# Three of four batches' experts sorted by token slots inside the MLP groups, instead of dense passes

## The reference

```python
x = x + tanh(g_xattn[0]) * two_way_attention(layernorm(x), ctx)   # with a sigmoid gate
x = x + tanh(g_ffn[0])   * experts(layernorm(x))                  # 8 linear experts, top 2
x = x + tanh(g_xattn[1]) * cross_attention(layernorm(x), ctx)
x = x + tanh(g_ffn[1])   * mlp(layernorm(x))                      # 256 -> 1024 -> 1024 -> 1024 -> 256

# experts: probs = softmax(x @ Wr); the two largest are taken, not renormalised
# out = sum over the two of  p_e * (x @ Wi[e]) @ Wo[e]
# mlp: h = silu(x@w1*s1) * (x@w2*s2); h = gelu(h@h1*s3); h = gelu(h@h2*s4); h @ w3 * s5
```

## Time and profile before

| what | value |
|---|---|
| runs | 1141.81, 1142.21, 1142.49 us (median 1142.21) |
| profiled execution | 1142.89 us, span 1141.0 us |
| PE busy | 1093.0 us (96%), 5194 products |
| DVE, ACT, POOL busy | 534.4, 439.9, 206.3 us |
| granted TensorE clock, mean | 0.983 |
| moved | 121.39 MB, mean 106 GB/s |

### The profile page before, as it was taken

How to read it: one execution, slowest core, us unless ns; L and a number is a source line. 1 busy time by engine, 2 the same in 40 slices (tenths; PEclk the granted TensorE clock), 3 DMA queues, 4 the chain that set the end, 5 groups by cost and what they waited for, 6 DMA issues and landing times.

```text
span 1141.0 us, 14295 instructions
## 1 busy us (share of the span) xinstructions
PE 1093.0 (96%) x5194; PEld 865.1 (76%) x5194; DVE 534.4 (47%) x1420; ACT 439.9 (39%) x820; POOL 206.3 (18%) x336
## 2 busy tenths in 40 slices
PE   7989979899999989999999999999999999999997
PEld 5757768677777767887887788788788788788886
DVE  6567666777777662243334235135135223332411
ACT  1344441112222244445435435535534443543531
POOL 0015552200000111121121122112112112112111
PEclk9989988999999989999999999999999999999999
DMA  9200000112222324443445345345444345443551
GB/s 342 99 1 1 1 1 1 37 56 74 74 74 75 128 61 116 137 148 111 129 120 157 113 127 166 111 136 151 117 131 148 111 129 149 128 115 116 176 146 40
DMA packets 32698, 121.39 MB, mean 106 GB/s; under 512 B 4222, under 2 KB 4478, under 8 KB 31736
## 3 DMA queue, kind: packets, MB, share of 16 engines
q0 software_dynamic: 25344, 92.29, 27.7%
q1 hardware_dynamic: 6456, 25.22, 6.6%
q10 hardware_dynamic: 832, 3.02, 0.7%
HBM read 116.31 MB, written 4.19 MB: 106 GB/s over the span
## 4 chain that ended last, share of the span: by engine, by line
PE 84%; DVE 6%; ACT 4%; issue 3%; POOL 1%; DMA 1%; DVEq 0%; SPq 0%; POOLq 0%; ACTq 0%
PE psum L849 53%; PE psum L728 13%; PE psum L751 2%; PE psum L738 1%; PE psum L463 1%; PE psum L550 1%; PE psum L526 1%; PE psum L777 1%; PE psum L759 1%; PE psum L706 1%; PE psum L564 1%; DVE x_residual L1539 1%; DMA x_residual<-in_x 1%; PE psum L580 1%; ACT L1118 1%
## 5 line engine op out<-in xcount | busy, mean ns | idle before, releaser
L849 PE MATMUL psum<-hidden_a_high,mlp_pieces 128*128 128x512 f32 x512 | 207.4, 405 | 0.0
L849 PE MATMUL psum<-hidden_b_high,mlp_pieces 128*128 128x512 f32 x512 | 200.6, 392 | 0.0
L849 PE MATMUL psum<-hidden_a_low,mlp_pieces 128*128 128x512 f32 x512 | 199.7, 390 | 0.0
L849 PE MATMUL psum<-hidden_b_low,mlp_pieces 128*128 128x512 f32 x512 | 199.2, 389 | 0.0
L1769 POOL DMA_DIRECT2D mlp_pieces<-in_mlp x176 | 94.5, 538 | 534.1 <-PE psum L849 528.3
L1653 DVE TENSOR_TENSOR hidden_a_low<-hidden_a,hidden_a_high 128x512 fp32r<-128x512 f32 x128 | 88.0, 688 | 173.8 <-ACT hidden_a_high L1170 173.0
L1653 DVE TENSOR_TENSOR hidden_b_low<-hidden_b,hidden_b_high 128x512 fp32r<-128x512 f32 x64 | 44.3, 693 | 221.0 <-ACT hidden_b_high L1170 221.0
L1539 DVE SCALAR_TENSOR_TENSOR x_residual<-psum,expert_weight,x_residual 128x256 f32 (+1 forms) x256 | 107.2, 476 | 41.1 <-PE psum L728 40.3
L849 PEld LDWEIGHTS psum<-hidden_a_high,mlp_pieces 128*128 128x128 f32 x512 | 96.2, 188 | 24.1 <-issue 3.6
L849 PEld LDWEIGHTS psum<-hidden_a_low,mlp_pieces 128*128 128x128 f32 x512 | 96.2, 188 | 22.1 <-issue 3.4
L849 PEld LDWEIGHTS psum<-hidden_b_low,mlp_pieces 128*128 128x128 f32 x512 | 96.2, 188 | 19.9
(11 more groups left out here) (211 smaller groups left out, 1624.5 us busy)
## 6 DMA issues: line engine op xcount, KB each, us to landing
mlp_pieces<-in_mlp POOLq DMA_DIRECT2D x176, 512.0 KB, 3.8
mlp_piece_to_examine<-in_mlp SPq DMA_DIRECT2D x22, 512.0 KB, 3.6
x_residual<-in_x SPq DMA_DIRECT2D x4, 1024.0 KB, 22.9
out<-x_residual SPq DMA_DIRECT2D x8, 512.0 KB, 3.4
expert_in<-in_Wi SPq DMA_DIRECT2D x1, 2048.0 KB, 16.7
expert_out<-in_Wo SPq DMA_DIRECT2D x1, 2048.0 KB, 21.3
attention_weights<-in_aw ACTq DMA_DIRECT2D x1, 1280.0 KB, 11.0
attention_weights<-in_aw ACTq DMA_DIRECT2D x2, 256.0 KB, 4.2
```

Source lines behind the costliest of these rows:

```text
L849: last = mm(o, a, b, start=(k == 0 and i == 0), stop=(k == n_k - 1 and i == len(parts) - 1))
```

## The change

Only batch 0 (groups 0 and 1, `ND` = 2) goes through the dense passes; the loop with passes 1 to 6 is gone. Batches 1, 2 and 3 (`NSB` = 3) are done inside MLP groups 0, 2 and 4 (`routed_in(n)`), with the batch that follows the one the MLP is at:

- In w12, DVE normalises the batch's eight tiles (`r_norm`, c = 0 to 3), PE transposes them in pairs (`r_turn`, c = 1 to 4) and makes the router logits in fp32 (`r_logits`, c = 2 to 5, `wrb`); DVE copies them (`r_copy`, c = 6), finds the two largest and marks them (`r_max`, c = 7, `r_mask` after the last low).
- In h1, PE makes the running count of tokens per expert with a triangular matrix (`r_rank`, after chunk 0); DVE makes each token's two weights (`r_coef`) and two slot numbers (`r_rank`, chunk 1, `r_tiles`, chunk 3). Each expert's slots are rounded up to tiles of 128: at most 23 tiles (`EB`) for 2048 slots. POOL writes each tile's normalised rows to the slots in HBM (`scatter`, 16 indirect DMAs of 128 rows of 1 KB, four ahead of each of the piece loads 6 to 9). The slot buffers, 3072 rows of 1 KB for each of three batches, are filled with zeros at the start by SP.
- In h2, SP loads the slots in chunks of four tiles into two buffers (`load_slots`). From chunk 1 on PE transposes pairs of slot tiles (`s_turn`) and, two pairs for each of the chunks 2 to 7, multiplies each tile with its own expert's matrix (`s_experts`), whose column is loaded from SBUF into a register (`s_columns`). ACT and DVE make high and low parts (`s_high`, `s_low`), ACT saves the result and issues its store to HBM (`s_save`).
- At the group's end POOL gathers each token's two rows for group n + 2, and inside group n + 1 for group n + 3 (`gather`, 8 indirect DMAs each); DVE adds them with their weights in group n + 1 (`add_rows`, `measure_rows`). In groups 1, 3 and 5 stage C is four chunks later (`turn_after`).
- The examination takes 16 pieces from three buffers and the last 6 from the ring itself. It lies in pass 0 and the last pass, and its result comes after the last pass.

```diff
-            with pe.Fori(0, NG // 2 - 1) as i:
-                b_pass(2 * i + 1, 1, 2 * i)
-                b_pass(2 * i + 2, 0, 2 * i + 1)
-            b_last_pass(NG - 1, 1)
+            b_last_pass(ND - 1, 1)
...
+                        if s is not None and 1 <= c <= 4:
+                            r_turn(s, c - 1)
+                        if s is not None and 2 <= c <= 5:
+                            r_logits(s, c - 2)
...
+                            if s is not None and layer == 0 and c == 0:
+                                r_rank(s)
+                            if s is not None and layer == 1:
+                                if c == 1:
+                                    columns = s_columns(s, 0)
+                                    s_turn(s * PAIRS)
+                                    s_turn(s * PAIRS + 1)
+                                for i in pairs_at(c):
+                                    if i == PAIRS // 2:
+                                        columns = s_columns(s, 1)
+                                    if i + 2 < PAIRS:
+                                        s_turn(s * PAIRS + i + 2)
+                                    s_experts(s * PAIRS + i, columns)
...
+                def s_experts(q, columns):
+                    pe.wait_ge(xsl_r, q + 1)
...
+                    for i in range(pair_tiles(q)):
+                        v = columns[(q % PAIRS * 2 + i) % 12]
+                        o = ps[:, 2 + q % 2, i * D:(i + 1) * D]
+                        t = slice(i * P, (i + 1) * P)
+                        for k in range(KC):
+                            mm(o, xsh[:, q % 2, k, t], wexp_h[:, k, bass.ds(v, D)], start=(k == 0), stop=False)
+                            mm(o, xsl[:, q % 2, k, t], wexp_h[:, k, bass.ds(v, D)], start=False, stop=False)
+                            last = mm(o, xsh[:, q % 2, k, t], wexp_l[:, k, bass.ds(v, D)], start=False,
+                                      stop=(k == KC - 1))
+                    last.then_inc(ye_ps, 1)
...
 # DVE's group, w12
+                        if s is not None and c < 4:
+                            r_norm(s, c)
+                        if s is not None and c == 6:
+                            r_copy(s)
+                        if s is not None and c == 7:
+                            r_max(s)
                     low(HC - 1, ha_f, ha_h, ha_l, 3 * HC * n + HC)
+                    if s is not None:
+                        r_mask(s)
...
 # POOL
+            def scatter(s, tiles):
+                for j in tiles:
+                    for i in range(2):
+                        pool.indirect_dma_start(
+                            slots[s], bass.IndirectOffsetOnAxis(ap=slot[:, s * JT + j, i:i + 1], axis=0),
+                            xm[:, j, :], None).then_inc(sc_done[s], 16)
...
+                    if s is not None and 6 <= piece < 10:
+                        if piece == 6:
+                            pool.wait_ge(ix_r, s + 1)
+                            pool.wait_ge(fill_done, 16 * NSB)
+                        scatter(s, (2 * piece - 12, 2 * piece - 11))
+                    if a is not None and piece == 8:
+                        pool.wait_ge(cb_r, JT * a + G)
+                        gather(n + 2)
...
+                if s is not None:
+                    for h in range(2):
+                        pool.wait_ge(st_done[h], 16 * NCK // 2 * (s + 1))
+                    gather(n + 2)
...
 # SP
+            def load_slots(s):
+                sp.wait_ge(sc_done[s], 16 * 2 * JT)
+                for c in range(NCK * s, NCK * (s + 1)):
+                    if c % NCK >= 2:
+                        sp.wait_ge(xt_ps, pairs_before(c - 2) + 2)
+                    n = chunk_tiles(c)
+                    sp.dma_start(xs[:, c % 2, 0:n, :], chunk_rows(slots, c, n)).then_inc(xs_in[c % 2], 16)
```

More of the change, by code:

```diff
@@ L52 @@
 RING = 6
+ND = 2
+NSB = B - 1
+EB = 23
+CHUNK = 4
+NCK = -(-EB // CHUNK)
+ROWS_B = NCK * CHUNK * P
+PAIRS = -(-EB // 2)
+XT0 = NT + G * ND
 SLICE = PIECE
@@ L157, in program @@
+        iota = place("weights", "tile_numbers", [1, EB])
+        eid = place("weights", "tile_expert_column", [1, NSB, EB], I32)
+        tri = place("weights", "triangle", [P, P])
+        slot = place("weights", "slots_of_tokens", [P, NSB * JT, 2], I32)
+        cab = place("weights", "weights_of_slots", [P, NSB * JT, 2])
         wk = room["work"][0]
@@ new lines, in r_logits @@
+                def r_logits(s, p):
+                    pe.wait_ge(rx_r, 4 * s + p + 1)
+                    if s == 0 and p == 0:
+                        pe.wait_ge(tri_in, 48)
+                    for i in range(2):
+                        j = 2 * p + i
+                        for k in range(KC):
+                            last = mm(ps[:, 0, j * E:(j + 1) * E], xmT[:, p % 2, k, i * P:(i + 1) * P],
+                                      wrb[:, k, :], start=(k == 0), stop=(k == KC - 1))
+                    last.then_inc(rl_b, 1)
@@ new lines, in s_columns @@
+                def s_columns(s, half):
+                    a, e = (0, 12) if half == 0 else (12, EB)
+                    pe.wait_ge(eid_r, s + 1)
+                    return nc.values_load_multi_w_load_instructions(
+                        eid[0:1, s, a:e], engines=[pe.engine], min_val=0, max_val=(E - 1) * D,
+                        skip_runtime_bounds_check_because="the column is a minimum with that of the last expert")[1]
+                def s_experts(q, columns):
+                    pe.wait_ge(xsl_r, q + 1)
+                    if q % PAIRS >= 2:
+                        pe.wait_ge(ye_r, q - 1)
+                    else:
+                        pe.wait_ge(xupc, 1 + G * (2 * (q // PAIRS) + 2))
+                    for i in range(pair_tiles(q)):
+                        v = columns[(q % PAIRS * 2 + i) % 12]
+                        o = ps[:, 2 + q % 2, i * D:(i + 1) * D]
+                        t = slice(i * P, (i + 1) * P)
+                        for k in range(KC):
+                            mm(o, xsh[:, q % 2, k, t], wexp_h[:, k, bass.ds(v, D)], start=(k == 0), stop=False)
[3 more added lines that the diff above has]
+                    last.then_inc(ye_ps, 1)
@@ new lines, in r_max @@
+            def r_max(s):
+                dve.wait_ge(lc_r, s + 1)
+                for j in range(JT):
+                    st.mark(dve.max(rtop[:, j, :], rlg[:, j, 0:E]))
+                st.wait()
+                dve.tensor_tensor(rlsub[:], rlg[:, :, 0:E], rtop[:, :, 0:1].broadcast_to([P, JT, E]), ALU.subtract
+                                  ).then_inc(le_r, 1)
+                st.link(dve.tensor_copy(rwant[:, :, 0:2], rtop[:, :, 0:2]))
+                for j in range(JT):
+                    st.mark(dve.match_replace(rmarked[:, j, :], rwant[:, j, :], rlg[:, j, :], TAKEN))
@@ L1637, in norm, with measure_rows @@
+            def measure_rows(g):
+                dve.wait_ge(cb_r, G * (g - 1))
+                for j in range(G):
+                    measure(G * g + j, j)
+                aggregate(G * g, G, 0, stats)
             def norm(n):
@@ L1703, in _ @@
             norm(0)
[L1704 removed]
+            b_end(ND - 1)
             steps_before = st.start + st.n
@@ L1866 @@
     d["out"] = nc.dram_tensor("out", (NG, P, G, D), F32, kind="ExternalOutput").ap()
+    for n in ("slots", "yrows"):
+        d[n] = [nc.dram_tensor(f"{n}_{b}", (ROWS_B, D), F32, kind="Internal").ap() for b in range(NSB)]
     program(nc, d)
```

446 lines of the change are left out of this document (377 added, 69 removed).

## The result

The changed kernel takes **1084.99 us** (median of 4 runs, 1082.92 to 1085.43) against 1142.01 (4 runs, 1141.37 to 1142.49). The ratio is 0.9497, 95% interval 0.9481 to 0.9514: 57.0 us gained. The profiled execution took 1084.55 us, its span is 1082.6. Forecast from 1142.89 was -62.1; it came to -58.3.

A forecast was written before the change was run, and what follows sets the result against it. PE (TensorE) was taken to bound the kernel. From 1142.89 us: -158.0 + 81.6 + 8.3 + 2 + 0 + 4.5 + 1 - 1.5 = -62.1, so 1080.8, forecast 1080; 1068 to 1092 at chance 0.50, 1064 to 1115 about 0.8.

The forecast's parts named there:

- The two sides of the sum: PE time removed with six dense passes, -158.0 us, against PE work added in three routed groups, +81.6 us.
- Six passes, -158.0: Six of eight dense passes go at 26.33 us each; pass 0 and the last, with its cross attention, stay.
- the ends, +1: Before the MLP: the weights' check sum now follows the last pass, mostly covered by DVE's norms releasing the turn; +1 us.
- 27.2 us of PE work a group, +81.6: Groups 0, 2 and 4: expert products, slot and x transposes, router logits and rank products on PE, 27.2 us each.
- DVE's r_max, +8.3: First h1 chunk: PE's k = 7 waits about 2.3 us for r_max, then 0.45 for r_mask; 2.75 in three groups.
- Clock, +2: PE, idle in the routed groups' stalls, can lose its clock: 0.7 us each, +2 in all, bounds 0 and 2.
- Slots, 0: Routing, scatter and slot load finish at T + 45, nearly 4 us before h2 wants them; S, POOL's indirect-DMA time, 1.1 us.
- one of the prediction's own signs of being wrong: Signs listed: expert products spaced near 0.2, PE idle before s_turn until slot rows come, or routed-group clock below 1.00.
- The 47 us: Scatters: extra cost if POOL were held 2.3 us for each whole indirect DMA; the prediction set it aside, citing the trace.
- Registers, +4.5: Expert products on PE: loading and addressing by weight-column registers costs 1.5 us a group, +4.5 in all.
- The w3 wait, -1.5: Between h2's last chunk and w3, the last two expert pairs cover PE's 0.50 us wait for DVE's low; -1.5 us.
- Gathers, hidden: POOL's 8 gathers for the even group and 8 for the odd one take 8.8 us, hidden, at no cost.

The follow-up runs named there:

- Experiments 2 and 9: 2: the changed kernel with the last dense pass's cross attention one step earlier, 1082.11 us; 9: its products earlier, turn left, memsets later, r_max and rank products moved, 1069.39 us.
- experiment 1: The changed kernel with r_max behind the first h1 chunk's last low part and the rank products one h1 chunk later: 1073.78 us, ratio 0.9407.
- experiment 4: The changed kernel with each expert product writing 128 columns instead of 256 (output not the reference's): 1079.93 us, ratio 0.9468.
- experiment 3: The changed kernel with expert products reading fixed weight columns and no register loads on PE (output not the reference's): 1084.64 us, ratio 0.9506.
- experiment 8: The changed kernel with a spare POOL operation of 1.07 us behind each of the 48 gathers: 1101.95 us, ratio 0.9655.
- The fast version: The changed kernel with r_max and rank products moved, last-pass cross attention products earlier with the turn left, and 10 memsets after DVE's step 1: 1069.39 us, ratio 0.9375.

## Why the prediction was right

It said 1080 for 1085.0, within its range. The two sides of the sum that carry it were right. That the miss is no larger is in part luck: several small terms were off in both directions and nearly cancel.

1. **Six passes, -158.0**. The MLP starts 153.5 earlier where 157.0 were summed. Two steps failed. One is that the last pass "stays" with its cross attention: the change moves it one step later, and PE then waits 1.4 us for probs_c, a wait that the last pass of before doesn't have. The other is "the ends, +1", that DVE's norms release the turn 2 us after PE's last product: 2.9 us are added there (9.16 for 6.30), since cross attention's update, a step later too, stands ahead of DVE's last additions, and PE waits 4.2 us. Experiments 2 and 9 move it back and bring 9.16 to 6.65 and 4.2 to 1.8. These two make 1.4 + 1.9 of the 3.5. The start itself varies by 3.7 us between executions, so the 3.5 alone would prove little; the two waits are the same in every trace.
2. **27.2 us of PE work a group, +81.6**. Confirmed by experiment 1: with the stall away a pair is 27.2 us longer than before. The spacing of 0.120 came true; in experiment 4 half the columns brought it to 0.1115 only.
3. **DVE's r_max, +8.3.** Right in place and kind, high in size: 1.77 us and up to 0.15, 1.8 to 1.9 a group instead of 2.75. `r_max` takes 2.2 us (280.02 to 282.20 in group 0) where 2.35 were summed; PE sees 1.77 of it and not 2.3, and of `r_mask` behind it up to 0.15 and not 0.45.
4. **Clock, +2.** The prediction took 0.7 a group. It is all or nothing: up to 1.8 us in groups 2 and 4 and hardly any in group 0, so 3.2 to 3.6 here, and by seven of 21 stalls about 1.8 for three on average (an estimate from these counts). Stall and clock together were put at 10.3 and are 11.2 by experiment 1, which also holds what the rank products gain (0.66 us in the chain behind the wait, 0.40 where they went). A clock below 1.00 in the routed groups is one of the prediction's own signs of being wrong; it showed, though the sum had 2 us for it.
5. **Slots, 0.** The cost was right (0.6), the slack of 4 us was not there. From T, the end of w12 (277.8 in group 0), the sum was T + 27.4 + 16 S. The slot numbers are ready at T + 16.7 and not 18.2 (-1.5). From there to the issue of the last scatter at 315.92 it is 21.4 us and not 18.1 (+3.3), mostly as S is 1.26 and not 1.1. That scatter has landed 2.6 us after its issue, where the sum has 1.1 + 3.8 (-2.3), and the slot chunk lands in 8.0 and not 3.8 (+4.2). 45.0 + 3.7 = T + 48.7: the first slot tile is there at 326.5, just when PE comes. The misses ate up the slack of nearly 4 us to the last half microsecond, and that they cost no more is luck. The step that failed is the load's 3.8 us, taken from the row of the piece loads, where no bunch of loads stands ahead. The 47 us that the prediction worked out from the Trainium skill (DMA: Bandwidth & Descriptors, "Anatomy of one DMA — SWDGE (gpsimd) path") are not what the runs show: the next such DMA starts on POOL after 1.26 us and not 2.3.
6. **Registers, +4.5.** Nothing, by experiment 3. Here the row on DVE, additions equally fast with a register, was the better guide than its load in the chain.
7. **The w3 wait, -1.5.** Waits of h2's and w3's products for DVE's low part (a row of 4.0 us before, 2.6 after): -1.4.
8. **Gathers, hidden.** True, with less room than it sounds: about 0.5 us each by experiment 8.

So of the 3.8 us by which the profiled execution missed the sum, 3.5 are the head, 1.7 the stretch behind the last work, which no step had, and the MLP gave 1.5 back: 4.5 of registers and 2.6 of r_max too much, clock, slots and small waits too little. Those with a number make -4.9 (registers -4.5, r_max -2.6, clock +1.5, slots +0.6, the w3 wait +0.1), and 1.0 us of waits for the batch's normalised rows (L1006), which no step had, come on top; the 2.4 us from there to -1.5 are not accounted for.

The fast version takes 15.6 us more off than the change as it stood; 11.2 of them are the item that the prediction had priced at 8.3 plus 2.

## What to carry to other kernels

When the bound engine runs at 99%, count its instructions at the spacing that the trace shows for their shape; the sum holds to a few per cent, and what is left lies in the small steps of another engine that are put ahead of its next input. Price such a step with the clock that its stall costs, and before moving it, look at the input of each thing that moves with it. A link that shows in the chain but ends just in time is worth nothing when made faster and its full time when made slower: test both sides before calling it slack. And read the whole change for what moves along with it: here one step in the last pass, left out of the description and the sum, made most of the 3.5 us by which the MLP started late.

## What the runs showed of the hardware

- An indirect DMA of 128 rows of 1 KB holds POOL 0.96 us (0.995 in the mean), and 0.30 us go by before the next one; a direct piece load takes 0.56.
- Products of 256 columns that read their weights' column from a register go at 0.120 us, as with a fixed one; products of 128 columns go at 0.1115 (experiment 4), so with a new weight load for each product half the columns gain 7%.
- Stalls of 1.8 us in PE, at the same place of the same work, were followed by some 3.4 us at 1.2 GHz (products 0.43 apart, 497.8 to 501.2 in group 2) in 7 of 21 cases, and not in the others: in the kernel after in groups 2 and 4 and not in group 0, in experiment 3 in group 2 alone, in experiment 4 in none.
- A 512 KB load that took 3.7 us with one other issued just ahead of it took 8.0 behind three, which POOL's queue had held back, with 344 to 410 GB/s moved meanwhile, where the mean of the whole execution is 147: read from the rows, not tested by moving the three.
